# Sixteen short sequences of attention and a gated recurrence: the softmax division moved from the token layout to the layout of the values product

## The chip, the cores and the metric

One core of one Trainium2 chip. The metric is the device time of one execution in microseconds (us), the median of several runs.

## The reference

For 16 sequences of 512 tokens with 256 features, fp32: sliding-window attention with 16 heads of 16 features (window 128, so each block of 128 queries sees its own and the previous block of keys, with a bias of slope times distance), a softmax, the output projection, the residual and a LayerNorm. Then a recurrence over the 16 sequences with 512 x 256 state, and at last a hidden layer for all sequences that needs the final state, with a second residual and LayerNorm:

```python
p = softmax(where(valid, q @ k.T / sqrt(16) + slope * delta, -inf));  o = p @ v
x = layernorm(x + o @ w_out.T)
f = sigmoid(x_t @ wf.T + c @ uf.T + bf); i = sigmoid(x_t @ wi.T + c @ ui.T + bi)
g = tanh(x_t @ wc.T + c @ uc.T + bc);    c = f * c + i * g
out = layernorm(x + tanh(x @ wo.T + c_final @ uo.T + bo))
```

## The kernel before

Everything is done in 3 passes of fp32r parts: each operand is split into a high part (ScalarE copies it with rounding, "hi") and a rest (VectorE or GpSimd subtracts, "lo"), and a product is hi*hi + hi*lo + lo*hi (`product` L916, and `abreast` L924, which runs two products beside each other on the upper and lower half of the rows).

The order is written out by hand: each engine has one function `iteration(t)`, and semaphores tie them. `iteration(t)` has 16 slots, `attend(0)` to `attend(15)`. On TensorE a slot issues `raw_scores(t, ...)` (L939) for four heads of a head group g = slot // 4 and `scores` (L961) for the slot seven earlier. VectorE (`maxima` L682) takes the row maxima of the raw scores, which stand in two PSUM banks; the raw scores of the next slot wait for them (`red_done`). ScalarE takes exponentials (`exps` L441), GpSimd masks them (`window` L343), and `values` (L977) multiplies with V. Maxima travel: `max_transpose` (L957), `max_row` (L450, ScalarE), `max_to_stack` (L257, two DMAs into the rows of Qs).

Three sequences are under way in one iteration: attention of t, the rest of the attention of t - 1 and its output of t - 2, gates of t - 3. Between slots TensorE does one other thing, in the four PSUM banks A0, A1, B0, B1 (they change roles each iteration, `pairs_of` L195): slot 0 `max_transpose`, `values(t-1, 1)`, a context transpose and the `o_transpose`s; slots 1, 2 gates; 3, 4 output projection; 5 values, context transpose, the first query/key pair of t + 1 (`project_qk`); 6, 7 gates; 8 values, context transpose; 9, 10 the values projection (`v_halves`); 11, 12 the second query/key pair (`qk_halves`); 13 `values(t, 0)`, context transpose, `x1_transpose`s; 14, 15 gates.

The values product of head group g is a bank of 128 rows (4 heads of 32 rows: 16 of context, one with the softmax denominator, the rest unused) by 512 tokens. `ctx_out` (L456, ScalarE) copies it to `ctx_raw`; `ctx_transpose` (L991) turns it in four 128 x 128 transposes to token rows; `normalise` (L693, VectorE) takes reciprocals and multiplies into `o_tok`. When all four groups are there `o_transpose` (L1024) turns `o_tok` back, four transposes for each of two chunks, and `ot_hi`/`ot_lo` split it to `oT` for the projection `project_out`/`out_halves`.

The DMA queue of SyncE (`iteration` L269) sends the query/key parts to DRAM (`parts_to_dram` L232, four DMAs for each of two chunks), fetches them replicated to the stacks Qs and Ks (`stack` L242, eight DMAs a head group, `stacked[g]`), moves the maxima, and loads and stores x, xt and x1. `x_hi`/`x_lo` split the transposed input for the sequence after next in slots 1 and 2; `x_lo` (L671) is on VectorE.

Before the loop the weights are split (`STAGED` L161, `weights_hi` L411, GpSimd L338 to L341). After it `last_sequences` drains the pipeline, and a second loop of 16 steps does the hidden layer.

## Time and profile before

| | us |
|---|---|
| median of 3 runs (lowest, highest) | 994.1 (992.67, 994.81) |
| the profiled execution | 994.83 |
| its span, first to last instruction | 992.7 |
| busy: TensorE, its weight loads, VectorE, ScalarE, GpSimd | 911.2, 749.7, 714.1, 574.8, 409.0 |
| mean granted clock of TensorE | 0.955 of full |

The profiled execution gives all durations; its own time is 2.1 us more than its span. "PEld" is the loading of weights on TensorE, one per matmul, and runs beside the previous matmul; the starts of these loads give the order and pace in which TensorE issues.

### The profile page before, as it was taken

To read this page: it belongs to the slowest core of one execution; us is meant where nothing else is said; L and a number is where in the kernel's file an instruction comes from. 1 tells how busy PE (TensorE), PEld (TensorE's weight loads), DVE (VectorE), ACT (ScalarE), POOL (GpSimd) and SP (SyncE) were. 2 spreads that over 40 slices of the span, in tenths; PEclk is the share of its full clock that TensorE was granted. 3 is DMA by queue.
4 is the path that set the end of the run, shared out by engine and by line. 5 is a ranking of instruction groups with operands and counts; after the bars stand their busy time and mean duration, and the time that the engine had idled before them with its cause. 6 is when DMAs were issued, how large, how long until landed. Compare 5 with 4: busy or idle time off the path is not lost. (4 is left out here: it accounts for less than half of the span.)

```text
span 992.7 us, 25986 instructions
## 1 busy us (share of the span) xinstructions
PE 911.2 (92%) x9500; PEld 749.7 (76%) x9500; DVE 714.1 (72%) x2795; ACT 574.8 (58%) x1167; POOL 409.0 (41%) x687
## 2 busy tenths in 40 slices
PE   3587889999999999999999999999999999989994
PEld 2365668888888888888888888888787876668884
DVE  7666677878787868787878787878787754337875
ACT  6044556565656565656565656565656554335786
POOL 6143343444535353535353535354444443001443
PEclk8586989999999999999999999999999989899998
DMA  7644454535454545353645454645444400131764
GB/s 265 164 124 127 131 139 132 151 122 156 124 151 128 145 134 150 123 154 125 153 128 151 128 143 137 149 131 147 133 121 138 119 23 22 44 106 46 215 204 131
DMA packets 93534, 131.86 MB, mean 133 GB/s; under 512 B 12128, under 2 KB 47584, under 8 KB 93408
## 3 DMA queue, kind: packets, MB, share of 16 engines
q1 hardware_dynamic: 93136, 129.95, 45.3%
q8 instruction: 76, 1.25, 0.5%
q14 instruction: 50, 0.41, 0.1%
q10 hardware_dynamic: 272, 0.26, 0.1%
HBM read 79.31 MB, written 50.33 MB: 131 GB/s over the span
## 5 line engine op out<-in xcount | busy, mean ns | idle before, releaser
L689 DVE CUSTOM_DVE_ANT_0 bank<-bank,mask 128x256 f32<-128x256 f32 (+1 forms) x1024 | 369.4, 423 | 130.7 <-PE bank L951 128.7
L448 ACT ACTIVATE Pt<-bank 128x512 f32<-128x512 f32 (+1 forms) x512 | 248.2, 536 | 193.4 <-PE bank L972 193.3
L347 POOL TENSOR_SCALAR_AFFINE_SELECT Pt<-Pt 128x512 f32<-128x512 f32 x256 | 170.4, 666 | 403.9 <-ACT Pt L448 403.9
L951 PE MATMUL bank<-Ks,Qs 59*128 59x256 f32 (+1 forms) x1024 | 148.2, 319 | 44.9 <-DVE max_q L689 31.3
L951 PEld LDWEIGHTS bank<-Ks,Qs 59*128 59x128 f32 x1024 | 107.3, 191 | 86.6 <-DVE max_q L689 42.5
L689 DVE DVE_READ_ACCUMULATOR2_ANT max_q<- 128x1 f32 x1024 | 144.9, 142 | 0.0
L349 POOL TENSOR_SCALAR_AFFINE_SELECT Pt<-Pt 128x384 f32<-128x384 f32 x256 | 144.7, 565 | 0.0
L986 PE MATMUL bank<-Pt,Vp 128*32 128x256 f32 (+1 forms) x2048 | 130.9, 377 | 0.0
L932 PE MATMUL bank<-x1T,Wg 64*128 64x512 f32 x960 | 127.9, 398 | 1.0 <-DVE o_tok L703 1.0
L932 PE MATMUL bank<-cT,Ug 64*128 64x512 f32 x960 | 125.7, 393 | 0.0
L972 PE MATMUL bank<-Qs,Ks 60*128 60x256 f32 (+1 forms) x1024 | 111.8, 271 | 0.7 <-ACT Pt L448 0.3
L986 PEld LDWEIGHTS bank<-Pt,Vp 128*32 128x32 f32 x2048 | 81.4, 116 | 31.9 <-issue 7.9
L932 PEld LDWEIGHTS bank<-cT,Ug 64*128 64x128 f32 x960 | 89.1, 184 | 18.2
L932 PEld LDWEIGHTS bank<-x1T,Wg 64*128 64x128 f32 x960 | 87.3, 185 | 18.9 <-DVE o_tok L703 1.4
L972 PEld LDWEIGHTS bank<-Qs,Ks 60*128 60x128 f32 x1024 | 94.7, 192 | 3.0 <-issue 1.3
L459 ACT ACTIVATE ctx_raw<-bank 128x512 f32<-128x512 f32 x64 | 38.2, 597 | 53.3 <-PE bank L994 50.7
L486 ACT ACTIVATE gate<-bank,bias_half 128x512 f32<-128x512 f32 x64 | 42.4, 685 | 42.2 <-PE bank L932 23.9
L920 PE MATMUL bank<-xT,Win 128*128 128x512 f32 x204 | 55.1, 423 | 7.9 <-DVE Win L661 7.9
L932 PE MATMUL bank<-Win,xT 64*128 64x256 f32 x768 | 54.6, 284 | 0.0
L920 PEld LDWEIGHTS bank<-xT,Win 128*128 128x128 f32 x204 | 40.1, 203 | 16.6 <-DVE Win L661 7.9
L661 DVE SCALAR_TENSOR_TENSOR qk_parts<-bank,qk_parts 128x512 fp32r<-128x512 f32 x64 | 42.5, 685 | 13.9 <-ACT qk_parts L431 13.9
L431 ACT ACTIVATE qk_parts<-bank 128x512 fp32r<-128x512 f32 x64 | 38.0, 593 | 23.0 <-PE bank L920 20.2
(111 smaller groups left out, 1354.7 us busy)
## 6 DMA issues: line engine op xcount, KB each, us to landing
parts_dram<-qk_parts SPq DMA_DIRECT2D x128, 256.0 KB
Qs<-parts_dram SPq DMA_DIRECT2D x128, 128.0 KB, 2.7
Ks<-parts_dram SPq DMA_DIRECT2D x128, 128.0 KB, 2.8
xt_raw<-in_xt SPq DMA_DIRECT2D x16, 512.0 KB, 4.5
Qs<-parts_dram SPq DMA_DIRECT2D x128, 64.0 KB, 2.7
Ks<-parts_dram SPq DMA_DIRECT2D x128, 64.0 KB, 2.7
x_res<-in_x SPq DMA_DIRECT2D x16, 512.0 KB, 3.9
x_dram<-y SPq DMA_DIRECT2D x16, 512.0 KB, 4.4
```

The source lines that it names most:

```text
L347: gp.affine_select(out=p4[:, :, 0:128], in_=p4[:, :, 0:128], compare_op=ALU.is_ge, fill=0.0, base=0, pattern=[[0, 4], [1, 128]], channel_m ...
L349: gp.affine_select(out=p4[:, 0:3, 128:256], in_=p4[:, 0:3, 128:256], compare_op=ALU.is_ge, fill=0.0, base=0, pattern=[[0, 3], [-1, 128]], ...
L448: sc.activation(probabilities(g, 2 * pair + odd)[:, S * a:S * a + n], SC[odd][:, 0:n], ACT.Exp).then_inc(exp_done, 1)
L459: sc.activation(ctx_raw[:, :], bank[:, :], ACT.Copy).then_inc(ctx_done, 1)
L486: ins = sc.activation(gate[:, k if k == 3 else which, :], bank[:, :], ACT.Tanh, bias=bias_half[:, which, j:j + 1], scale=0.5)
L661: return ve.scalar_tensor_tensor(out_, in_, scale, hi.bitcast(F32), op0=ALU.mult, op1=ALU.subtract)
L689: ins = ve.tensor_tensor_reduce(out=raw, in0=raw, in1=mask[:, keys], scale=1.0, scalar=MASKED, op0=ALU.add, op1=ALU.max, accum_out=max_q[: ...
L920: ins = te.matmul(out_, w, m, start=(first and n == 0), stop=(last and n == len(todo) - 1))
L932: ins = te.matmul(out_, w(r), m(r), start=(turn == 0 and opens and n == 0), stop=final, skip_group_check=True)
L951: ins = te.matmul(MX[odd][:, 256 * (n % 2):256 * (n % 2) + 256][:, keys], Qs[rows, 2 * g + pair, n * WIN:(n + 1) * WIN], Ks[rows, 2 * g + ...
L972: ins = te.matmul(SC[odd][:, 256 * (j % 2):256 * (j % 2) + width], Ks[rows, 2 * g + pair, j * WIN:(j + 1) * WIN], Qs[rows, 2 * g + pair, j ...
L986: ins = te.matmul(bank[32 * hh:32 * hh + 32, j * WIN:j * WIN + width], Vp[:, j, PITCH * h:PITCH * h + 32], probabilities(g, hh)[:, 256 * j ...
```

## The change

Division happens in the layout of the values product, for all sequences but the last (whose old path stays, as `last_ctx_transpose`, `last_normalise`, `last_o_transpose`, `last_ot_hi`, `last_ot_lo`):

- `ctx_out` waits for its own copy and sends `ctx_raw` to DRAM (`ctx_dram`) from ScalarE's queue.
- SyncE loads the contexts back as `o_un`, 128 rows of context a chunk (`load_contexts`), and the denominators as `den_q` (`load_denominators`, four DMAs). VectorE transposes `den_q` in blocks, inverts, transposes back; SyncE stores the inverses and loads them replicated over the 16 rows of each head as `inv_den`; GpSimd multiplies (`scale_contexts`). `ot_hi` and `ot_lo` read `o_un` from SBUF.
- `ctx_transpose`, `normalise` and `o_transpose` go.
- `x_hi`/`x_lo` are now for t + 2, in slots 13 to 15, and `x_lo` is on GpSimd, between its windows 1 and 2 of group 1.
- The values projection and the second query/key pair change places (slots 9, 10 and 11, 12) and banks; slots 0, 13 and 14 use the other pair of banks, and in slot 13 the x1 transposes come ahead of `values(t, 0)`.
- `parts_to_dram(t, 1)` moves from the end of iteration t - 1 behind `stack(t, 1)` of iteration t; `max_to_stack(t, 0)` ahead of `stack(t, 2)`.
- Wo and Uo take the place of Win in SBUF and are loaded and split at the end of the loop.

```diff
@@ SyncE
+            def load_denominators(t):
+                sp.wait_ge(den_cleared, 1)
+                for g in range(QUADS):
+                    wait(sp, ctx_stored[g], 16, t, 16)
+                wait(sp, inv_stored, 16, t - 1, 16)
+                rows = ctx_dram[t % 2].rearrange("g (h r) (q i) -> q (g h) r i", r=2 * D, i=128)[:, :, D, :]
+                for q in range(4):
+                    sp.dma_start(den_q[32 * q:32 * q + H, :], rows[q]).then_inc(den_in, 16)
+            def load_contexts(t, c):
+                for g in (2 * c, 2 * c + 1):
+                    wait(sp, ctx_stored[g], 16, t, 16)
+                wait(sp, otlo_done, 2, t - 1, c + 1)
+                rows = ctx_dram[t % 2, 2 * c:2 * c + 2].rearrange("g (h r) s -> (g h) r s", r=2 * D)[:, 0:D, :]
+                sp.dma_start(o_un[:, c, :], rows).then_inc(o_un_in[c], 16)
+            def store_inverses(t):
+                wait(sp, inv_turned, 1, t, 1)
+                sp.dma_start(inv_dram[t % 2].rearrange("r (q i) -> q r i", i=128), den_q[:, :]).then_inc(inv_stored, 16)
+            def spread_inverses(t):
+                wait(sp, inv_stored, 16, t, 16)
+                for c in range(KC):
+                    wait(sp, scaled_done, 2, t - 1, c + 1)
+                    rows = inv_dram[t % 2, 8 * c:8 * c + 8]
+                    sp.dma_start(inv_den[:, c, :], rows.unsqueeze(1).to_broadcast([8, D, S])).then_inc(inv_in[c], 16)
...
+                by_rows = p1 and t - 1 < B - 1
                 if p1: max_to_stack(t - 1, 3)
-                if now: stack(t, 1)
+                if now:
+                    stack(t, 1)
+                    if t: parts_to_dram(t, 1)
...
+                if by_rows: load_contexts(t - 1, 0)
                 if real(t + 2): load_xt(t + 2)
                 if now:
+                    max_to_stack(t, 0)
                     stack(t, 2)
-                    max_to_stack(t, 0)
                     stack(t, 3)
...
+                if by_rows: load_denominators(t - 1)
                 if n1: stack(t + 1, 0)
+                if by_rows: load_contexts(t - 1, 1)
                 if now: max_to_stack(t, 2)
-                if n1: parts_to_dram(t + 1, 1)
+                if by_rows:
+                    store_inverses(t - 1)
+                    spread_inverses(t - 1)
+                if t == B - 1: load_last_weights()
@@ GpSimd
+                if p2 and t - 2 < B - 1:
+                    for c in range(KC):
+                        scale_contexts(t - 2, c)
                 if p1:
...
+                    for hh in range(2):
+                        window(t, 1, hh)
+                    if real(t + 2):
+                        for c in range(KC):
+                            x_lo(t + 2, c)
+                    for hh in range(2, 4):
                         window(t, 1, hh)
@@ ScalarE
                 sc.activation(ctx_raw[:, :], bank[:, :], ACT.Copy).then_inc(ctx_done, 1)
+                if t < B - 1:
+                    wait(act, ctx_done, 4, t, g + 1)
+                    sc.dma_start(ctx_dram[t % 2, g], ctx_raw[:, :]).then_inc(ctx_stored[g], 16)
...
                 attend(10)
+                if n1: qk_hi(t + 1, 2, A0)
                 attend(11)
-                v_out(t, 0, A0)
+                if n1: qk_hi(t + 1, 3, A1)
                 attend(12)
-                v_out(t, 1, A1)
-                if n1: qk_hi(t + 1, 2, B0)
-                max_row(t, 2, A0)
+                v_out(t, 0, B0)
+                v_out(t, 1, B1)
+                if p2: x1_hi(t - 2, 0, A0)
+                max_row(t, 2, B0)
                 attend(13)
-                if n1: qk_hi(t + 1, 3, B1)
-                ctx_out(t, 0, A1)
-                if p2:
-                    x1_hi(t - 2, 0, B0)
-                    x1_hi(t - 2, 1, B1)
+                if p2: x1_hi(t - 2, 1, A1)
+                ctx_out(t, 0, B1)
+                if real(t + 2): x_hi(t + 2, 0)
                 attend(14)
+                if real(t + 2): x_hi(t + 2, 1)
@@ VectorE
                 attend(10)
+                if n1: qk_lo(t + 1, 2, A0)
                 attend(11)
+                if n1: qk_lo(t + 1, 3, A1)
                 attend(12)
-                if n1: qk_lo(t + 1, 2, B0)
                 attend(13)
-                if n1: qk_lo(t + 1, 3, B1)
-                if p1: normalise(t - 1, 3, A0)
-                if p2:
-                    x1_lo(t - 2, 0, B0)
-                    x1_lo(t - 2, 1, B1)
+                if p1:
+                    turn_denominators(t - 1)
+                    invert_denominators(t - 1)
+                if p2: x1_lo(t - 2, 0, A0)
+                if p1: turn_inverses(t - 1)
+                if p2: x1_lo(t - 2, 1, A1)
@@ TensorE
                 attend(9)
-                v0, v1 = v_halves(t, 0, A0), v_halves(t, 1, A1)
+                if n1: q2, q3 = qk_halves(t + 1, 2, A0), qk_halves(t + 1, 3, A1)
...
                 attend(11)
-                if n1: q2, q3 = qk_halves(t + 1, 2, B0), qk_halves(t + 1, 3, B1)
+                v0, v1 = v_halves(t, 0, B0), v_halves(t, 1, B1)
...
                 attend(13)
+                if p2:
+                    x1_transpose(t - 2, 0, A0)
+                    x1_transpose(t - 2, 1, A1)
                 wait(pe, v_done, 2, t, 1)
-                max_transpose(t, 2, A0)
-                values(t, 0, A1)
+                max_transpose(t, 2, B0)
+                values(t, 0, B1)
...
                 if p2:
-                    g0, g1 = gate_halves(0, A0, state_first=True), gate_halves(1, A1, state_first=True)
-                    wait(pe, o_done, 4, t - 1, 4)
+                    g0, g1 = gate_halves(0, B0, state_first=True), gate_halves(1, B1, state_first=True)
+                    wait(pe, maxrow_done, 4, t, 3)
                     wait(pe, ctx_done, 4, t, 1)
```

## Rows read from the trace of the kernel before

**Rows 1.** The page: busy time, and the granted clock in 40 slices.
```profile
PE 911.2 (92%) x9500; PEld 749.7 (76%) x9500; DVE 714.1 (72%) x2795; ACT 574.8 (58%) x1167; POOL 409.0 (41%) x687
...
PE   3587889999999999999999999999999999989994
```
**Rows 2.** Busy time by stretches: stretch, its length, engines, clock, DMA share, GB/s.
```profile
510.00:558.00 48.00, 47.52 (x555) 39.63 (x559) 36.99 (x154) 29.48 (x63) 22.87 (x38) 1.00 0.49 145
```
**Rows 3.** Waits from 160 to 760 us: total, times, longest.
```profile
POOL Pt L347 <- ACT Pt L448: 273.8, 72, 5.3
...
PEld bank L951 <- DVE max_q L689: 13.2, 41, 0.6
```
**Rows 4.** Timeline of PEld around the transposes: start, duration, what, count.
```profile
496.97 0.42 PEld L994 LDWEIGHTS bank<-ident,ctx_raw 128*128 128x128 f32 x4 [0.20 <-issue]
497.56 0.30 PEld L951 LDWEIGHTS bank<-Ks,Qs 59*128 59x128 f32 x4 [0.17 <-issue]
...
510.03 0.42 PEld L1040 LDWEIGHTS bank<-ident,y 128*128 128x128 f32 x4 [0.35 <-DVE qk_parts L661]
...
513.76 0.43 PEld L951 LDWEIGHTS bank<-Ks,Qs 59*128 59x128 f32 x4
...
517.03 0.43 PEld L951 LDWEIGHTS bank<-Ks,Qs 59*128 59x128 f32 x4
...
519.60 0.42 PEld L994 LDWEIGHTS bank<-ident,ctx_raw 128*128 128x128 f32 x4 [0.20 <-issue]
...
521.07 0.30 PEld L951 LDWEIGHTS bank<-Ks,Qs 59*128 59x128 f32 x4 [0.17 <-issue]
...
534.49 0.42 PEld L994 LDWEIGHTS bank<-ident,ctx_raw 128*128 128x128 f32 x4 [0.20 <-issue]
534.88 2.60 PEld L920 LDWEIGHTS bank<-xT,Win 128*128 128x128 f32 x12
...
546.83 0.42 PEld L994 LDWEIGHTS bank<-ident,ctx_raw 128*128 128x128 f32 x4 [0.20 <-issue]
```
**Rows 5.** Timeline of PEld, raw scores of slots 10 to 13.
```profile
500.35 0.29 PEld L951 LDWEIGHTS bank<-Ks,Qs 59*128 59x128 f32 x3 [0.58 <-DVE max_q L689]
...
502.11 0.42 PEld L951 LDWEIGHTS bank<-Ks,Qs 59*128 59x128 f32 x4
...
504.36 0.29 PEld L951 LDWEIGHTS bank<-Ks,Qs 59*128 59x128 f32 x3 [0.30 <-DVE max_q L689]
...
504.71 1.33 PEld L932 LDWEIGHTS bank<-xT,Win 64*128 64x128 f32 x12
...
506.32 0.29 PEld L951 LDWEIGHTS bank<-Ks,Qs 59*128 59x128 f32 x3 [0.15 <-DVE max_q L689]
```
**Rows 6.** Timelines of ACT and DVE: qk_hi, qk_lo, the residual.
```profile
506.57 0.60 ACT L431 ACTIVATE qk_parts<-bank 128x512 fp32r<-128x512 f32 x1 [0.19 <-PE bank L932]
...
507.20 0.69 DVE L661 SCALAR_TENSOR_TENSOR qk_parts<-bank,qk_parts 128x512 fp32r<-128x512 f32 x1 [0.94 <-ACT qk_parts L431]
...
533.91 1.28 DVE L715 TENSOR_TENSOR y<-bank,x_res 128x512 f32<-128x512 f32 x2
```
**Rows 7.** POOL's subtraction by line; landing of stack's DMAs (L254); an issue of SP.
```profile
L364 POOL TENSOR_TENSOR cT<-c,cT x26: 1265/1280/1301, 199.7 to 798.4; 128x512 fp32r<-128x512 f32 x26
...
DMA to landing us min/median/max: 2.0/2.7/5.9
...
499.29 0.44 SPq L285 DMA_DIRECT2D x_dram<-y  x1
```
**Rows 8.** Timelines of POOL and DVE at the start of the kernel.
```profile
21.56 1.44 POOL L340 TENSOR_TENSOR Wo<-Pt,Wo 128x512 fp32r<-128x512 f32 x1
22.96 3.42 POOL L340 TENSOR_TENSOR Ug<-gate,Ug 128x1536 fp32r<-128x1536 f32 x1
...
23.04 5.57 DVE L661 SCALAR_TENSOR_TENSOR cT<-c,cT 128x512 fp32r<-128x512 f32 x2 [1.16 <-ACT cT L613]
```
**Rows 9.** Stretch of 10 us near the end, columns as in rows 2.
```profile
870.00:880.00 10.00, 8.02 (x39) 6.64 (x38) 5.44 (x14) 3.58 (x7) 1.68 (x4) 0.83 0.00 0
```

More of the change, by code:

```diff
@@ L70, in build @@
         rden = sb("rden", [128, 16])
-        o_tok = sb("o_tok", [128, NB, E])
+        o_un = sb("o_un", [128, KC, S])
+        inv_den = sb("inv_den", [128, KC, S])
+        den_q = sb("den_q", [128, 128])
+        den_t = sb("den_t", [128, 128])
+        last_o_tok = sb("last_o_tok", [128, NB, E])
         oT = sb("oT", [128, 2, KC, S], F32R)
@@ L161, in build @@
         STAGED = ((Wout, w_stage[:, 1536:2048]), (Wg, w_stage[:, 2048:3584]),
-                  (Wo, w_stage[:, 3584:4096]), (Ug, gate[:, 0:3, :].rearrange("p a b -> p (a b)")), (Uo, ctx_raw[:, :]))
+                  (Ug, gate[:, 0:3, :].rearrange("p a b -> p (a b)")))
         def real(t):
@@ L364, in c_lo, with x_lo, scale_contexts @@
                 gp.tensor_tensor(cT[:, 1, j, :], c2[:, j, :], cT[:, 0, j, :].bitcast(F32), ALU.subtract).then_inc(clo_done, 1)
+            def x_lo(t, c):
+                wait(pool, xhi_done, 2, t, c + 1)
+                gp.tensor_tensor(xT[:, t % 2, 1, c, :], xt_raw[:, c, :], xT[:, t % 2, 0, c, :].bitcast(F32), ALU.subtract).then_inc(xlo_done, 1)
+            def scale_contexts(t, c):
+                wait(pool, o_un_in[c], 16, t, 16)
+                wait(pool, inv_in[c], 16, t, 16)
+                gp.tensor_tensor(o_un[:, c, :], o_un[:, c, :], inv_den[:, c, :], ALU.mult).then_inc(scaled_done, 1)
             def iteration(t):
                 p1, p2, now = real(t - 1), real(t - 2), real(t)
+                if p2 and t - 2 < B - 1:
+                    for c in range(KC):
+                        scale_contexts(t - 2, c)
                 if p1:
@@ L384, in iteration @@
                         window(t, 0, hh)
-                    for hh in range(4):
+                    for hh in range(2):
[4 more added lines that the diff above has]
+                    for hh in range(2, 4):
                         window(t, 1, hh)
@@ L389, in _ @@
                 iteration(t)
+                if t == B:
+                    for n, w in enumerate((Wo, Uo)):
+                        pool.wait_ge(last_hi, n + 1)
+                        gp.tensor_tensor(w[:, 1, :, :], out_stage[:, n, :].rearrange("p (c n) -> p c n", c=KC),
+                                         w[:, 0, :, :].bitcast(F32), ALU.subtract).then_inc(last_lo, 1)
             def second(t, rnd, i):
@@ L605, in _ @@
             for k in range(4):
-                qk_hi(0, k, banks[4 + (k + 2) % 4])
-            act.wait_ge(weights_in, 80)
-            for n in range(5):
+                qk_hi(0, k, banks[4 + k])
+            act.wait_ge(weights_in, 48)
+            for n in range(3):
                 weights_hi(n)
@@ L762, in iteration @@
                 attend(0)
-                if p1: normalise(t - 1, 0, A0)
-                if p2:
-                    ot_lo(t - 2, 0, B0)
-                    ot_lo(t - 2, 1, B1)
-                attend(1)
-                if n1: x_lo(t + 1, 0)
-                if p3: forget(t - 3, 0)
-                attend(2)
-                if n1: x_lo(t + 1, 1)
+                if p3: forget(t - 3, 0)
+                attend(1)
+                if t == 0: x_lo(1, 0)
+                attend(2)
+                if t == 0: x_lo(1, 1)
+                if p2:
+                    ot_lo(t - 2, 0)
+                    ot_lo(t - 2, 1)
                 attend(3)
@@ L989, in values, with last_ctx_transpose @@
                 ins.then_inc(pv_ready, 1)
-            def ctx_transpose(t, g, bank):
-                wait(pe, ctx_done, 4, t, g + 1)
+            def last_ctx_transpose(g, bank):
+                wait(pe, ctx_done, 4, B - 1, g + 1)
                 for n in range(NB):
@@ L1217, in last_sequences @@
                 values(t, 2, MX[1])
[L1218 removed]
+                last_ctx_transpose(1, MX[0])
                 wait(pe, gate_done, 6, t - 2, 3)
@@ L1224, in last_sequences @@
                 scores(t, 3, 2)
-                wait(pe, o_done, 4, t, 2)
-                ctx_transpose(t, 2, MX[0])
+                pe.wait_ge(o_done, 2)
+                last_ctx_transpose(2, MX[0])
                 scores(t, 3, 3)
@@ L1236, in last_sequences @@
                 gate_of_input(t - 1, 1, A1)
-                wait(pe, o_done, 4, t, 3)
-                ctx_transpose(t, 3, MX[0])
+                pe.wait_ge(o_done, 3)
+                last_ctx_transpose(3, MX[0])
                 gate_of_state(t - 1, 0, A0)
```

237 lines of the change are left out of this document (129 added, 108 removed).

## The prediction

> **What bounds the kernel now.** I read the page first: TensorE (PE) is busy for 92% of the span, and between the first and the last slices every slice reads 9 [rows 1]. The table by stages then shows one 48 us stretch of the steady state: PE 47.5 us busy at granted clock 1.00, VectorE (DVE) 37.0, ScalarE (ACT) 29.5, POOL 22.9, the DMA engines at half [rows 2]. So what PE issues sets the pace. The waits of 160 to 760 us say how tightly: PE's weight loads (PEld) waited only 13.2 us for DVE's maxima [rows 3]. The order of these loads is the schedule. A sequence is 16 slots (the attends 0 to 15); the context transposes of slot 8 come at 496.97 and, a sequence later, at 546.83, so the period is 49.9 us [rows 4]. A full slot with gate products takes 3.27 (513.76 to 517.03 [rows 4]). The reader is to see in rows 4 what follows the transposes, and in rows 5 that slots 9 to 13 are different from the rest: there PE has little to do between two raw scores, and the loop raw scores, maxima, next raw scores sets the pace: 2.25 us for an odd slot (502.11 to 504.36), 1.96 for an even one (504.36 to 506.32).
>
> **What PE loses.** Per sequence: 16 context transposes and 8 of o_tok. Slot 0 has four and eight: 519.60 to 521.07, 1.47 us. Slot 8 has four and the change of operand behind them: 496.97 to 497.56, 0.59. In slot 5 four cost 534.49 to 534.88, 0.39, slot 13 the same [rows 4]. But in slot 5 the query/key product that follows goes into the bank that the residual reads: that addition starts at 533.91, and two take 1.28 [rows 6], so the bank is free at 534.6 and 0.28 is saved, not 0.39. In slot 13 the x1 transposes also waited 0.35 for qk_lo [rows 4], which now comes two slots earlier. Together 1.47 + 0.59 + 0.39 + 0.28 + 0.35 = 3.08 us a sequence. This is the ceiling of the gain.
>
> **What PE gets back as waits.** First the swap. The query/key pair now closes in slot 10 instead of 12, and DVE has qk_lo behind maxima 10 and 11. Today the chain reads: raw loads 504.36, product loads 504.71 to 506.04, ACT copy from 506.57, DVE qk_lo 507.20 to 507.89 [rows 5, 6]: 3.53 us from the raw loads to its end. Today only x1 transposes stand behind it. Then it is maxima 11 that stands behind it on DVE, and raw scores 12 on PE wait for those: 3.53 + (2.25 - 0.53, the lag from loads to the reader) = 5.25 us from raw 10 to raw 12, against 504.36 - 500.35 = 4.01 now: +1.24. The second qk_lo (0.69) stands before maxima 12 where the lag of 0.53 covers most: +0.16. I take 1.4 (the chain is the nearest row there is: the same instructions, two slots later); the bounds are 0 (DVE takes both in gaps) and 2 x (0.69 + 0.60) = 2.6, both copies and both subtractions in full.
>
> Second, slot 13 now ends with values(t, 0) in B1, and slot 14's gate product needs B1 empty. The copy starts 0.53 after the last load (506.04 to 506.57) and takes 0.60 [rows 5, 6]: 1.13. PE spends 0.20 on the change of operand [rows 4] and 0.35 on the scores (504.36 to 504.71) before it asks for the bank: wait 0.58. ACT is then still at the second x1 copy, which stands behind the exponentials of slot 13: half a copy more, 0.27. I take 0.85, bounds 0.58 and 1.18 (a whole copy ahead).
>
> Third, slots 0 to 3. ACT has copies of the gates, the exponentials, the context copy, its wait for that copy and a DMA issue, then ot_hi. With slot 0 shortened, the scores of slot 1 reach ACT's exponentials earlier than they end: 0.1. ot_lo of both chunks now stands between maxima 2 and 3 and reads o_un and oT, both in SBUF. Here the trace shows how POOL and DVE disturb each other: two DVE subtractions with both inputs in SBUF took 5.57 us from 23.04 while POOL ran a tensor_tensor of 3.42 from 22.96 [rows 8]; such an operation with one input in PSUM takes 0.69 [rows 6]. So DVE was held until POOL's was over. The Trainium skill ("SBUF — State Buffer", section "SBUF: two separate sides") has it that the pair of ports is an exclusive lock for the whole instruction; by that rule forget waits behind scale_contexts too, and the trace agrees. I charge 0.15 for ot_lo behind the windows; forget (slot 0) may lose up to one POOL operation, 1.28 [rows 7], but slot 1 is a slot of 3.27 with gate products as cover, so 0; without them it would be 1.28. Sum of this part 0.25, bounds 0 and 1.3.
>
> **What costs nothing, and why.** x_lo leaves DVE for POOL (two of 1.28 [rows 7]) between windows 1 and 2 of group 1; POOL sat idle 273.8 us of 600 before its windows [rows 3]. The values of slot 0 need these windows: they come last on POOL behind both x_lo, and the cover is thin, a few tenths. scale_contexts adds two more; the next windows are wanted in slot 5. If these covers went, it would be 1.28 for each x_lo. DVE loses four reciprocals, four multiplications and two x_lo, gains two transposes and one reciprocal: it is not the bound except in slots 9 to 13. ACT issues four DMAs, 0.44 each if they are like SP's [rows 7], in its idle time. DMA: 1 MB written and 1 MB read more a sequence on 7 MB, at a share of 0.49 [rows 2]. SP gets nine more issues; parts_to_dram(t, 1) moves behind stack(t, 1), wanted at slot 8; load_contexts(t-1, 0) holds SP until ot_lo in slot 2, then max_to_stack(t, 0) goes ahead of stack(t, 2), still three slots ahead of its use in slot 8. stack(t, 1) has to land before slot 4, which comes 1.5 us sooner than now, since slot 0 is shorter; its DMAs land after 2.7 [rows 7]. I put nothing down for it, as no wait for a DMA is among the large ones now; it is the cover that I know least.
>
> **The sum.** Steady state: -3.08 + 1.4 + 0.85 + 0.25 = -0.58 us a sequence, in 13 of them: -7.5. Iterations 1 and 2, at a partly lower clock and already waiting for DVE: -0.6 each, -1.2. Start: POOL has no longer Wo's 1.44 ahead of Ug [rows 8], and DVE is released to maxima 0 that much sooner: -1.4 (bounds 0 and 3.1). End: eight o_tok transposes less (1.47 - 0.39 = 1.1), three copies of the last weights (0.60 each) ahead of the layernorm that PE waits for: +0.7. Total -9.4. The profiled execution took 994.8 us (span 992.7), 0.7 above the median of 994.1. 994.8 - 9.4 = 985.4, or 984.7 from the median: I say **985**. With every wait at its low end the steady state gives 13 x (0.58 - 3.08) = -32.5, at its high end 13 x (2.6 + 1.18 + 1.3 - 3.08) = +26: 960 to 1018 with the -1.9 of both ends of the kernel. All at an end together is improbable; the forecast's own range is 974 to 996.
>
> **Rivals.** (1) *The waits are mostly covered*, DVE taking qk_lo in the pauses it has before each raw score in slots 9 to 13. For it: those pauses are 0.5 us and the period is otherwise PE's. Against: maxima 11 is in order behind it. Gain 2 to 3.08 a sequence: 994.1 - 1.9 - 13 x 3.08 = 952, or 966. Chance 0.27. (2) *The inverses land late.* After turn_inverses in slot 13: an issue 0.44, a landing 2.7, two issues 0.9, a landing 2.7 [rows 7]: 6.7 us; two slots of 3.27 and the wait of 0.85 later, at 7.4, POOL is ready for them. Its two multiplications take 2.56, ACT wants the result some 4.5 us after slot 0 began: margin about 2. With both landings at the longest, 5.9, the chain is 6.4 longer and 4 late; ot_hi then holds the exponentials of slot 2, and scores 3 and the output product wait. A third of that, 1.3 us a sequence, is what slots 2 and 3 can't hide if only one of the landings is long: 985 + 17 = 1002. It decides once the two landings take over some 7.5 us together. Chance 0.13. The Trainium skill ("DMA: Bandwidth & Descriptors", section "Why a DMA increments its semaphore by 16 and not by 1") says that a DMA is spread over the largest number up to 16 that divides both slowest dimensions; the inverse store's is 4, and the spreads' 8, so by it this would be the case to come. No row here shows engines by DMA. (3) *The clock falls*, the slower side. Where PE was busy for 8.0 of 10 us the granted clock was 0.83, a third of the time at 1.2 instead of 2.4 GHz [rows 9]. Slots 10 to 14 would have some 2 us of idle time in 12. One such drop each sequence costs up to 1.7 us: 985 + 13 x 1.7 = 1007. Against: with slots 9 to 13 as they are, the clock stays at 1.00 [rows 2]. It decides if the idle time lies together. Chance 0.10. (4) *Nothing in the net*: 992 to 996, the returned waits equal the removed work, 0.05. The forecast has 0.45.
>
> **How the numbers follow.** 0.2% of 994 is 2 us, about what a measurement can tell from no change. Faster: the forecast below 992 (0.38), rival 1 (0.27), a little of 2: 0.67. Same: 0.09. Slower: rivals 2 and 3 and the upper end of the forecast, 0.24. The range from 952 to 1007 leaves out the end of either side.
>
> **What would show it.** The period by raw-score loads: 49.3 by the forecast, 47 by rival 1. Right: slot 0 near 2.5 us, no ctx_transpose; a wait of PEld L951 for DVE's maxima of over 1 us in slot 12; a wait of PE for ACT's ctx_raw of about 0.8 in slot 14; granted clock 1.00. Rival 2 shows as POOL's scale waiting for DMA inv_den and PE for oT in slot 3; rival 3 as a clock below 1 in the steady slices. Wrong altogether: the slots 11 to 13 as short as now, or SP late with stack(t, 1) at slot 4 (PE waiting for Ks, Qs from parts_dram).

## The result, and the profile after

The changed kernel takes 1056.02 us (median of 4, 1053.76 to 1057.9), the kernel before in the same comparison 994.45 us (median of 4): ratio 1.0615, 95% interval 1.058 to 1.0649. The prediction was 985 with a range from 952 to 1007: the sign is wrong, and the time lies 49 us beyond the slower end. The profiled execution has a span of 1054.3 us, 61.6 more than before. Here and below a ratio leaves out runs that lie over 1.5% above the fastest run of their kernel (one of four in e2, three of twelve in e12; in e3 it would leave a single run, so none is given).

The page after, busy time and slices (columns as in [rows 1]):

```profile
PE 900.7 (85%) x9140; PEld 741.6 (70%) x9140; DVE 692.8 (66%) x2693; ACT 578.3 (55%) x1167; POOL 487.9 (46%) x745
...
PE   3587789898989898979898989899897989789995
...
PEclk9677789998989998989899999999999989899998
```

TensorE has 360 instructions and 10.5 us of work less (911.2 [rows 1]), and its idle time went from 81.5 us (992.7 - 911.2) to 153.6: its share of the span fell from 92% to 85%. The slices, which read 9 everywhere before, alternate between 8 and 9, and the granted clock does the same. A wait that recurs once a sequence looks like this. The waits of 160 to 800 us name it (engine, line, waited for: total, times, longest):

```profile
PEld bank L1042 <- DVE y L838: 54.8, 12, 6.1
DVE y L838 <- DMA x_res<-in_x: 48.8, 12, 5.6
POOL o_un L432 <- DMA inv_den<-inv_dram: 20.0, 21, 2.4
PEld bank L1094 <- DMA Qs<-max_rows: 7.1, 9, 1.8
```

TensorE waits in slot 5 with the query/key projection (L1042) for the bank that the residual (L838) reads, and the residual waits 4.1 us a time, in all twelve sequences, for x_res, the input rows that it adds. I priced the inverses, which are late by less than 1 us a time, and not this. SyncE's timeline of one iteration shows why x_res is late, first before, then after:

```profile
518.95 1.36 SPq L262 DMA_DIRECT2D Qs<-max_rows  x2
...
524.12 0.43 SPq L275 DMA_DIRECT2D x_res<-in_x  x1
```

```profile
446.00 1.38 SPq L275 DMA_DIRECT2D Qs<-max_rows  x2
447.48 2.60 SPq L267 DMA_DIRECT2D Qs<-parts_dram  x4
450.12 1.82 SPq L267 DMA_DIRECT2D Ks<-parts_dram  x4
452.06 3.51 SPq L252 DMA_DIRECT2D parts_dram<-qk_parts  x4
455.62 1.50 SPq L326 DMA_DIRECT2D x_res<-in_x  x1
457.24 1.29 SPq L293 DMA_DIRECT2D o_un<-ctx_dram  x1
```

Before, x_res came right behind `stack(t, 1)`, 5.2 us after the issue of the maxima; now the four DMAs of `parts_to_dram(t, 1)`, 256 KB each, stand between, and it is 9.6 us. Being issued later is only half of it. The page's lists of DMA issues give size and median time from issue to landing, first before, then after:

```profile
x_res<-in_x SPq DMA_DIRECT2D x16, 512.0 KB, 3.9
```
```profile
x_res<-in_x SPq DMA_DIRECT2D x16, 512.0 KB, 8.0
```

The same 512 KB land 4.1 us later after their issue when 1 MB of stores is ahead in the queue. So x_res loses 4.4 us at the issue and 4.1 us on the way. As the wait that is left is 4.1 us, about 4.4 of the 8.5 were slack.

The rest of the loss is the clock. Four stretches around one such wait (columns as in [rows 2]):

```profile
450.00:460.00 10.00, 9.95 (x140) 8.39 (x136) 7.49 (x34) 5.21 (x11) 5.27 (x9) 1.00 0.65 179
460.00:466.00 6.00, 0.26 (x1) 0.26 (x2) 1.00 (x2) 0.60 (x1) 0.00 (x0) 0.93 0.95 271
466.00:472.00 6.00, 6.00 (x20) 4.39 (x22) 1.88 (x10) 0.60 (x1) 1.68 (x4) 0.50 0.63 109
472.00:482.00 10.00, 10.00 (x119) 8.15 (x119) 9.20 (x34) 7.30 (x16) 4.33 (x7) 1.00 0.55 152
```

TensorE does almost nothing for 6 us (0.26 of 6.00) while the DMA engines are busy at 0.95, and is then granted 0.50, the 1.2 GHz level, for the next 6 us. The twelve loads of the query/key projection behind this wait take 4.77 us where the same twelve took 2.60 [rows 4] (over sequences 3 to 14 it is 3.57 to 4.77, on average 4.40):

```profile
465.74 4.77 PEld L1042 LDWEIGHTS bank<-xT,Win 128*128 128x128 f32 x12 [6.06 <-DVE y L838]
```

The period is read as before, from the starts of the raw-score loads: means over sequences 3 to 14, by slot. Slots 2, 3, 4, 6 and 9, left out, changed by less than 0.1.

| slots | 5 | 7 | 8 | 10 | 11 | 12 | 13 | 14 | 15 | 0 | 1 | period |
|---|---|---|---|---|---|---|---|---|---|---|---|---|
| before | 6.08 | 3.28 | 3.16 | 2.54 | 1.83 | 2.07 | 4.63 | 3.13 | 3.27 | 4.03 | 3.36 | 49.95 |
| after | 12.04 | 3.27 | 2.58 | 2.38 | 3.10 | 2.29 | 3.86 | 3.57 | 3.35 | 2.59 | 3.15 | 54.77 |

4.83 us a sequence in these twelve is 57.9 of the 61.6 in the span; 5.0 more were lost before sequence 3, and 1.4 came back behind sequence 14. Slot 5 alone lost 5.95; everything else together gained 1.12.

### The profile page after: what moved, and what is told of

The parts are those of the page before. It is cut to its first block and busy times, and to the rows that moved or that the text cites. A ratio compares the mean times of both kernels' runs of the same rounds, so it can differ in the third digit from the quotient of the medians.

```text
span 1054.3 us, 25331 instructions
## 1 busy us (share of the span) xinstructions
PE 900.7 (85%) x9140; PEld 741.6 (70%) x9140; DVE 692.8 (66%) x2693; ACT 578.3 (55%) x1167; POOL 487.9 (46%) x745
## 2 busy tenths in 40 slices
DMA packets 114232, 164.77 MB, mean 156 GB/s; under 512 B 14588, under 2 KB 52924, under 8 KB 114108
## 5 line engine op out<-in xcount | busy, mean ns | idle before, releaser
L1073 PE MATMUL bank<-Ks,Qs 59*128 59x256 f32 (+1 forms) x1024 | 151.2, 323 | 49.3 <-DVE max_q L794 32.4
L407 POOL TENSOR_SCALAR_AFFINE_SELECT Pt<-Pt 128x384 f32<-128x384 f32 x256 | 147.4, 576 | 0.0
L1042 PE MATMUL bank<-xT,Win 128*128 128x512 f32 x204 | 79.1, 563 | 60.4 <-DVE y L838 51.8
L1108 PE MATMUL bank<-Pt,Vp 128*32 128x256 f32 (+1 forms) x2048 | 127.6, 372 | 3.1 <-POOL Pt L407 3.1
L1042 PEld LDWEIGHTS bank<-xT,Win 128*128 128x128 f32 x204 | 56.4, 285 | 78.1 <-DVE y L838 55.3
L1054 PEld LDWEIGHTS bank<-cT,Ug 64*128 64x128 f32 x960 | 92.8, 184 | 20.4 <-issue 5.2
L1054 PEld LDWEIGHTS bank<-x1T,Wg 64*128 64x128 f32 x960 | 91.2, 185 | 12.8 <-issue 0.3
L412 POOL TENSOR_SCALAR var_eps<-mean_var 128x4 f32<-128x4 f32 x16 | 3.8, 240 | 132.3 <-DVE mean_var L849 132.2
L426 POOL TENSOR_TENSOR xT<-xt_raw,xT 128x512 fp32r<-128x512 f32 x28 | 35.9, 1291 | 58.3 <-ACT xT L507 58.3
L838 DVE TENSOR_TENSOR y<-bank,x_res 128x512 f32<-128x512 f32 x32 | 20.7, 686 | 57.6 <-DMA x_res<-in_x 51.7
```

Of the source, the lines that this page charges most:

```text
L407: gp.affine_select(out=p4[:, 0:3, 128:256], in_=p4[:, 0:3, 128:256], compare_op=ALU.is_ge, fill=0.0, base=0, pattern=[[0, 3], [-1, 128]], ...
L426: gp.tensor_tensor(xT[:, t % 2, 1, c, :], xt_raw[:, c, :], xT[:, t % 2, 0, c, :].bitcast(F32), ALU.subtract).then_inc(xlo_done, 1)
L1042: ins = te.matmul(out_, w, m, start=(first and n == 0), stop=(last and n == len(todo) - 1))
L1054: ins = te.matmul(out_, w(r), m(r), start=(turn == 0 and opens and n == 0), stop=final, skip_group_check=True)
L1073: ins = te.matmul(MX[odd][:, 256 * (n % 2):256 * (n % 2) + 256][:, keys], Qs[rows, 2 * g + pair, n * WIN:(n + 1) * WIN], Ks[rows, 2 * g + ...
L1108: ins = te.matmul(bank[32 * hh:32 * hh + 32, j * WIN:j * WIN + width], Vp[:, j, PITCH * h:PITCH * h + 32], probabilities(g, hh)[:, 256 * j ...
```

## The experiments

The queue theory: the DMAs that SyncE issues are served in the order of issue; the change puts bulk (parts, contexts) ahead of transfers on which TensorE or VectorE depends within a slot or two. Its rivals: the loss is the swap and the bank waits on the engines, or it is the additional bytes, whichever queue they take. In all, twelve kernels ran; ratios are to the kernel before on the same chip, whose medians were 993.4 to 995.6 and, for e4 to e6, 996.2. The expected times came true in e7 and e12 alone; e9 missed by 1.9 us, e3 with three of its four runs, the others by more.

**e1: x_res ahead of the parts** (in the kernel after)

```diff
                 if now:
                     stack(t, 1)
-                    if t: parts_to_dram(t, 1)
                 if p2:
                     wait(sp, y_done, 2, t - 3, 2)
                     sp.dma_start(x_res[:, :, :], x[t - 2].rearrange(tok, p=128)).then_inc(xres_in, 16)
+                if now and t: parts_to_dram(t, 1)
```


> The changed kernel with the x_res load issued ahead of parts_to_dram(t, 1) instead of behind it, nothing else. Queue theory (the load stands in SyncE's queue behind 1 MB of stores, is issued some 4 us later and lands after 8.0 us instead of 3.9, and the residual of slot 5 waits for it): the landing goes back to 4 to 5 us, the wait of DVE y for DMA x_res (51.7 us in 13) goes to nearly 0, slot 5 from about 12 us to about 6, the time to 975 to 985. Traffic theory (the 33 MB added by contexts and inverses slow every load): the landing stays at 6 us or more, and the time stays above 1030.

Measured: 1023.24 us, 1.0285 (1.0257 to 1.0313), where 975 to 985 was expected. Slot 5 is down to 5.82, x_res lands after 4.4 us, and half of the loss is gone; the other half is not. A new wait stands in its place, in slot 7 (6.60 instead of 3.27):

```profile
PEld bank L1093 <- DMA Qs<-max_rows: 34.6, 17, 3.9
```

**e2: parts(t + 1, 1) back at the end of the iteration**, behind the inverses (in the kernel after)

```diff
                     stack(t, 1)
-                    if t: parts_to_dram(t, 1)
...
                     spread_inverses(t - 1)
+                if n1: parts_to_dram(t + 1, 1)
```


> The changed kernel with parts_to_dram(t + 1, 1) at the end of iteration t again (behind spread_inverses). Queue theory: as e1, 975 to 985, unless max_to_stack(t, 3) now waits for the stores, which would show as PE waiting for Qs from max_rows. Traffic theory: above 1030, since no byte is gone.

Measured: 1038.6 us, 1.04 (1.0309 to 1.0491). The place of before is no longer the same place: the end of the iteration now holds the waits for the inverses, so the parts go out late. In one iteration maxima 3 are issued at 442.56, right behind the parts (438.27, 4.09 for four); before, 6.4 us lay between (559.05 and 3.33, then 568.80). TensorE waits for maxima (36.1 us) and for the stack's keys (16.3). The time alone is what the traffic theory had (above 1030).

**e3: the kernel before with only that move**

```diff
-                if now: stack(t, 1)
+                if now:
+                    stack(t, 1)
+                    if t: parts_to_dram(t, 1)
...
-                if n1: parts_to_dram(t + 1, 1)
```


> The kernel before with one part of the change alone: parts_to_dram(t, 1) behind stack(t, 1) of iteration t, ahead of the x_res load. Queue theory: the load is issued 3.5 us later and lands after about 8, so 1.5 to 2 us after the residual wants it: 1010 to 1030. Traffic theory: nothing is added here, so no change, 992 to 997.

Measured: 1038.75 us (median; its runs spread from 1021.59 to 1045.3, too far for a ratio), before 993.4. The same wait in the kernel before, from this line alone, in the run of 1038.2 us that was profiled:

```profile
DVE y L716 <- DMA x_res<-in_x: 28.0, 12, 4.1
```

x_res lands after 8.4 us instead of 3.9, slot 5 grows from 6.08 to 9.09, the period to 53.15. Nothing of the new division is in this kernel: the move alone costs 28 us by the fastest run and 45 to 52 by the other three, so from about half to five sixths of the loss. Why the fastest run is 17 us below the others is not shown; within the profiled one slot 5 varies from 7.1 to 11.6.

**e4: e1, and the DMAs of the maxima issued by ScalarE** in `max_row` instead of SyncE

```diff
@@ SyncE, max_to_stack
-                wait(sp, maxrow_done, 4, t, g + 1)
-                for odd in range(2):
...
+                return
@@ ScalarE, max_row
+                wait(act, maxrow_done, 4, t, g + 1)
+                for odd in range(2):
+                    r = 64 * odd + ROW_MAX
+                    sc.dma_start(Qs[r:r + 1, 2 * g:2 * g + 2, :].bitcast(F32),
+                                 max_rows[8 * odd:8 * odd + 8, :].bitcast(F32)).then_inc(maxrow[g], 16)
```


> The kernel of e1 with the two DMAs of max_to_stack issued by ScalarE behind its own copy instead of by SyncE; same bytes, same DMA engines, another queue. Queue theory (PE's waits for Qs from max_rows, 34.6 us in 17 in e1, come from 8 KB standing behind 1 to 1.8 MB in SyncE's queue, landing after 7 to 9 us): these waits go, the time to 980 to 990. Traffic theory (the DMA engines themselves are too busy): they stay, and the time stays within 1% of e1's 1023.

Measured: 1062.12 us, 1.0661 (1.0635 to 1.0688). The waits for max_rows are gone (0.4 us in 1), as the queue theory has it, though in a kernel that is itself slower; but ScalarE now issues eight small DMAs a sequence between its exponentials and stands behind its own waits:

```profile
L534 ACTq DMA_DIRECT2D Qs<-max_rows x128: 627/633/2536, 41.4 to 886.1; - x128
```
```profile
ACT Pt L524 <- issue: 79.4, 47, 3.3
```

So an issue of 0.63 us and the wait ahead of it cost more on ScalarE than the late landing did.

**e5: e1, with SyncE's small transfers ahead of its large ones**

```diff
-                if by_rows: load_contexts(t - 1, 0)
-                if real(t + 2): load_xt(t + 2)
                 if now:
                     max_to_stack(t, 0)
                     stack(t, 2)
-                    stack(t, 3)
-                if n1: parts_to_dram(t + 1, 0)
+                if by_rows: load_contexts(t - 1, 0)
+                if now: stack(t, 3)
+                if real(t + 2): load_xt(t + 2)
                 if now: max_to_stack(t, 1)
+                if n1: parts_to_dram(t + 1, 0)
```


> The kernel of e1 with SyncE's order changed: max_to_stack(t, 0) and stack(t, 2) ahead of load_contexts(t - 1, 0), load_xt behind stack(t, 3), max_to_stack(t, 1) ahead of parts_to_dram(t + 1, 0). Queue theory: waits for Qs from max_rows fall from 34.6 us to under 10, time 983 to 995. Traffic theory: within 1% of e1's 1023.

Measured: 1018.81 us, 1.0225 (1.0194 to 1.0255). Slots 5 and 7 are as they should be (5.82, 3.28), and the wait has moved on, to slot 15 (5.60) and, in some sequences, 11, with the same total; 983 to 995 was expected:

```profile
PEld bank L1093 <- DMA Qs<-max_rows: 34.5, 21, 3.1
DVE den_t L800 <- DMA den_q<-ctx_dram: 22.4, 13, 3.0
```

**e6: e5, and both qk_lo of the second pair behind maxima 12** (VectorE)

```diff
-                if n1: qk_lo(t + 1, 2, A0)
                 attend(11)
-                if n1: qk_lo(t + 1, 3, A1)
                 attend(12)
+                if n1: qk_lo(t + 1, 2, A0)
+                if n1: qk_lo(t + 1, 3, A1)
```


> The kernel of e5 with VectorE's two qk_lo of the second query/key pair behind the maxima of slot 12 instead of behind those of slots 10 and 11. If the term of the prediction is right (qk_lo ahead of maxima 11 costs TensorE 1.4 us in slots 11 and 12), slots 11 and 12 together fall from 5.3 us to about 4, and the time by 13 x 1.2 = 16 us against e5, less what the x1 transposes then wait for the banks (up to 0.7 a sequence): 6 to 16 us faster than e5. If the slots are long for another reason (ScalarE's copies), no change.

Measured: 1022.75 us, 1.0289 (1.0233 to 1.0344). Slots 11 and 12 fell from 5.28 (in sequences without a DMA wait) to 4.13, 1.15 of the 1.4 that my prediction put there; slot 14 took 0.77 back, and the period stayed (51.18 after 51.21). The gain of 6 to 16 us that was expected did not come. The swap's cost is real and of the size forecast, but it is not where the 61 us are.

**e7: the kernel after without the trip**. Contexts are neither stored nor loaded, denominators and inverses neither, and SyncE has its order of before. It leaves out the attention output (o_un keeps a constant); the splits, the multiplications on GpSimd, the transposes of VectorE, the swap and TensorE's order are all there.

```diff
@@ SyncE
-                if by_rows: load_contexts(t - 1, 0)
-                if by_rows: load_denominators(t - 1)
-                if by_rows: load_contexts(t - 1, 1)
-                    store_inverses(t - 1)
-                    spread_inverses(t - 1)
@@ GpSimd, scale_contexts
-                wait(pool, o_un_in[c], 16, t, 16)
-                wait(pool, inv_in[c], 16, t, 16)
+                wait(pool, otlo_done, 2, t - 1, c + 1)
@@ ScalarE, ctx_out
-                    sc.dma_start(ctx_dram[t % 2, g], ctx_raw[:, :]).then_inc(ctx_stored[g], 16)
```


> The changed kernel without the trip through DRAM: contexts, denominators and inverses are neither stored nor loaded (o_un and inv_den hold ones, so the attention output is left out of the result), and SyncE has the order of before; all compute of the change stays. If TensorE's share of the prediction is right (period 49.3 with qk_lo's 1.4 us and slot 14's 0.45 in it, some 2.4 to 2.7 us less than before in slots 0, 5, 8 and 13), the time is 955 to 975, and the whole loss of the change lies in DMAs. If the loss lies in the new order of the engines, 985 or more.

Measured: 973.48 us, 0.9779 (0.9761 to 0.9796). Waits of 160 to 800 us:

```profile
PEld bank L1064 <- DVE max_q L783: 20.9, 49, 1.4
...
PEld bank L1085 <- DMA Qs<-max_rows: 4.8, 7, 1.2
```

No wait for x_res, and the period is 48.20: on the engines the change does gain, 1.74 us a sequence. All of the loss, 82 us between e7 and the kernel after, belongs to the trip and to SyncE's order. This refutes the first rival.

**e8: e6 with still more of SyncE's order changed**: maxima 2 ahead of `stack(t + 1, 0)`, parts(t + 1, 1) between the store and the spread of the inverses, and the first half of `x1_lo` ahead of the denominators (the inverses are turned behind both halves)

```diff
-                if now and t: parts_to_dram(t, 1)
...
-                if n1: stack(t + 1, 0)
                 if by_rows: load_contexts(t - 1, 1)
                 if now: max_to_stack(t, 2)
-                if by_rows:
-                    store_inverses(t - 1)
-                    spread_inverses(t - 1)
+                if n1: stack(t + 1, 0)
+                if by_rows: store_inverses(t - 1)
+                if n1: parts_to_dram(t + 1, 1)
+                if by_rows: spread_inverses(t - 1)
```


> The kernel of e6 with parts_to_dram(t + 1, 1) sent while SyncE otherwise waits for the stored inverses, max_to_stack(t, 2) ahead of stack(t + 1, 0), and the first x1_lo ahead of the turned denominators. Queue theory: each small DMA then has little ahead of it; PE's waits for Qs from max_rows fall from 32 us to under 12, slot 14 goes back to 3.6, time 975 to 1000. If the added bytes themselves cost the time wherever they stand, 1010 or more.

Measured: 1100.05 us, 1.1044 (1.1022 to 1.1066), the slowest of all:

```profile
POOL o_un L430 <- DMA inv_den<-inv_dram: 158.9, 22, 15.4
ACT oT L551 <- POOL o_un L430: 115.5, 22, 10.7
...
PEld bank L1092 <- DMA Qs<-max_rows: 5.3, 6, 1.9
```

The maxima are on time (5.3 us), and now it is the inverses that stand behind 1 MB. They hold GpSimd, GpSimd holds ot_hi, ot_hi holds ScalarE's exponentials and so the scores of slot 3 (11.02 instead of 2.02). That is the chain of my rival 2, with the place right, and at a price of 9.0 us a sequence instead of 1.3.

**e9: the kernel before, with ScalarE storing each context bank to DRAM** (nobody reads it): 1 MB a sequence, in a queue of its own

```diff
+                pt, pg = before(t, g)
+                wait(act, ctx_stored[pg], 16, pt, 16)
                 sc.activation(ctx_raw[:, :], bank[:, :], ACT.Copy).then_inc(ctx_done, 1)
+                wait(act, ctx_done, 4, t, g + 1)
+                sc.dma_start(ctx_dram[t % 2, g], ctx_raw[:, :]).then_inc(ctx_stored[g], 16)
```


> The kernel before with one thing added: ScalarE stores each copied context bank to DRAM (1 MB a sequence on its own queue), and nobody reads it. Queue theory (only SyncE's queue order matters): within 0.5% of before, 990 to 999. Byte theory (what is on the 16 DMA engines delays the small DMAs): 1005 or more, with PE waiting for Qs from max_rows.

Measured: 1000.86 us, 1.0059 (1.0044 to 1.0074). A quarter of a megabyte behind each context copy, its four issues and ScalarE's waits for them cost 5.7 us in all, 1.9 more than the queue theory allowed. The stores' bytes cannot be the 61 us.

**e10 and e11: the loads of contexts, x_res and xt_raw issued by ScalarE** (three loads of bulk and the second half of the contexts, four issues a sequence), the maxima left with SyncE: e10 on the order of e5, e11 on SyncE's order of the kernel after

```diff
@@ ScalarE
                 max_row(t, 0, A0)
+                load_contexts(t - 1, 0)
...
                 if n1: qk_hi(t + 1, 1, B1)
+                if real(t + 2): load_xt(t + 2)
                 attend(7)
+                if p1: load_x(t - 1)
...
                 if p3: c_hi(t - 3, 1)
+                load_contexts(t - 1, 1)
                 attend(10)
```


> e1_xres_first plus the order of e5_small_first, and the loads of contexts, x_res and xt_raw issued by ScalarE (four issues a sequence) instead of SyncE; the maxima stay with SyncE. Queue theory: what SyncE held up (x_res, then the maxima of slots 11 and 15) is no longer behind these loads, the period falls from 51.2 towards the 48.2 of e7_no_trip, ScalarE pays 4 x 0.6 of which half shows: 49.5, in all 990 to 1000. Rival, the bytes (4 MB more traffic each way makes every landing longer, whichever queue): x_res and the maxima still land late, 1015 or more.

> The kernel after, SyncE's order kept as the change has it, only the loads of contexts, x_res and xt_raw issued by ScalarE. Queue theory: the wait of the residual for x_res (48.8 us in 12) goes to nothing, x_res has half a sequence to land; 512 KB of loads less stand between parts and maxima 0, so at most a wait of 1 to 2 us in slot 7: period 50.5, 1005 to 1015 against 1056. Rival, the bytes: 1040 or more.

Measured: e10 1028.98 us, 1.0359 (1.0316 to 1.0402); e11 1061.46 us, 1.0657 (1.0616 to 1.0698). Both missed, e11 by 46 us, and by their numbers the rival had both. (The "4 MB more traffic each way" of the first is a slip: the trip adds 1 MB each way a sequence.) The waits say more. In e11 none is left for x_res, slot 5 is 5.82, and one slot has nearly all that the period is above e7's, 5.45 of 5.89 us: slot 11 (8.35), with this wait:

```profile
PEld bank L1109 <- DMA Qs<-max_rows: 61.8, 12, 6.7
```
```profile
480.86 2.50 SPq L252 DMA_DIRECT2D parts_dram<-qk_parts  x4
483.99 1.36 SPq L275 DMA_DIRECT2D Qs<-max_rows  x2
```

Maxima 1 stand directly behind the 1 MB of parts(t + 1, 0), as in the kernels before and after, but here ScalarE's loads of xt and x_res, another 1 MB, run at the same time. Two stretches around these issues:

```profile
480.00:484.00 4.00, 4.00 (x55) 3.09 (x56) 3.60 (x17) 4.00 (x10) 0.00 (x0) 1.00 1.08 244
484.00:488.00 4.00, 3.56 (x44) 2.69 (x38) 3.43 (x15) 3.40 (x7) 3.60 (x5) 1.00 1.08 281
```

The DMA share reads 1.08: all engines are taken, by both queues, and the maxima, issued at 483.99, hold TensorE until 493.47. In the kernel after, behind the same parts, the share is 0.62 in the 4 us around their issue (480 to 484), and all its waits for maxima together are 7.1 us. So the rival is half right. By these rows a transfer waits for what is ahead in its own queue (e1, e3) and also for what the other queue has under way. The Trainium skill ("DMA: Bandwidth & Descriptors", section "Issuing engines are not separate DMA queues") says that DMAs of all issuing engines run on the same 16 DMA engines and interleave, and that issuing from several engines saves only the time of the issue; the share in these rows agrees with the first half. My expectation had freed the first transfer in the queue and not gone on to the next. Not all of the wait is the maxima's, though: ScalarE is held here as well, its exponentials start again at 491.66, behind its own load of the contexts ("ACT Pt L523 <- issue", 60.4 us in 24). In e10 the parts stand behind the maxima, and slot 11 (4.49) is lost otherwise: ScalarE, in order, waits in slot 9 for the store of group 3 to land before it can issue the load of the contexts, and its exponentials wait behind that (its row "ACT Pt L522 <- issue" has 39.0 us in 24).

**e12: e10 with three steps moved**

```diff
@@ ScalarE
-                load_contexts(t - 1, 1)
                 attend(10)
...
                 if real(t + 2): x_hi(t + 2, 1)
+                load_contexts(t - 1, 1)
                 attend(15)
@@ SyncE
+                if by_rows: load_denominators(t - 1)
                 if p2:
                     wait(sp, x1_done, 4, t - 2, 4)
                     sp.dma_start(x1_dram[t - 2].rearrange(tok, p=128), y[:, :, :]).then_inc(x1_out, 16)
-                if by_rows: load_denominators(t - 1)
@@ VectorE
+                if p2: x1_lo(t - 2, 0, A0)
                 if p1:
                     turn_denominators(t - 1)
                     invert_denominators(t - 1)
-                if p2: x1_lo(t - 2, 0, A0)
-                if p1: turn_inverses(t - 1)
                 if p2: x1_lo(t - 2, 1, A1)
+                if p1: turn_inverses(t - 1)
```


> e10_bulk_act_queue with three steps moved: ScalarE loads the second half of the contexts in slot 14 instead of slot 9 (there it held ScalarE and so the scores of slot 11), SyncE loads the denominators ahead of the store of x1 instead of behind it, and VectorE subtracts the first half of x1 ahead of the denominators. Queue theory: slot 11 falls from 4.71 to 3.1 and slot 14 from 4.14 to 3.6, the period from 51.2 to 49.0, in all 990 to 1000, about the kernel before; better than before only if slot 7 has no wait left. Rival, the bytes: the waits turn up at another transfer, 1015 or more.

Measured: 993.25 us (median of 12, 987.87 to 1008.03), before 995.32 (17): 0.9983 (0.9954 to 1.0012) and 1.001 by the means of all runs, so no difference that can be told. Against the kernel after that is some 63 us less, with the same 25331 instructions and the same 164.77 MB:

```profile
span 986.1 us, 25331 instructions
...
DMA packets 114232, 164.77 MB, mean 167 GB/s; under 512 B 14588, under 2 KB 52924, under 8 KB 114108
```
```profile
POOL o_un L425 <- DMA inv_den<-inv_dram: 35.1, 22, 7.0
...
PEld bank L1108 <- DMA Qs<-max_rows: 8.5, 5, 3.5
...
PEld bank L1087 <- DMA Ks<-parts_dram: 6.3, 6, 1.9
```

This is the run that decides about the bytes. By the times alone their rival had e2, e5, e8, e10 and e11; but with every byte of the trip moved the kernel comes within 20 us of e7, which moves none of them, so that is the most that they cost as such; the other 63 of the 82 are the order and the issuing engine. The profiled run is the fastest of the twelve. Its period is 48.87. Of the 0.66 that this is above e7, 0.42 is slot 7, in five sequences of twelve, where the raw scores of slot 8 wait for the keys: the queue is still late at times. Its runs spread by 20 us, more than those of any kernel here but e3. GpSimd waits up to 7.0 us for the inverses here, and ScalarE for GpSimd in turn only 2.1 us in 4. By the rule of the Trainium skill cited under e11, nothing should come of the second queue but issue time. Here e5, with one queue, takes 1.0225 of before and e12 0.9983; but e12 has more moved than the queue, and e10, which has the queue and not the three steps, takes 1.0359, so that the queue's own share of the 2.4% is not separated.

## Why the prediction was wrong

**The step that failed** is the sentence under "What costs nothing": "parts_to_dram(t, 1) moves behind stack(t, 1), wanted at slot 8". I asked when the moved step is wanted and what it is moved behind, but not what it is moved ahead of. Between its new place and the next wait stand x_res, 512 KB that the residual wants in slot 5. The term was 0. By e3, the kernel before with this move alone, it is 3.20 us a sequence (53.15 - 49.95) in a run of 1038.2 us, and by the fastest run some 2.2 (28/13, an estimate); in the kernel after, where slot 0 is shorter by 1.44 and so slot 5 comes sooner, slot 5 is 6.22 longer than in e7. About 4.2 of this is the late transfer (54.8/12, less the 0.36 that this wait has in e7 too), about 1.8 the slow clock behind it (4.40 - 2.60). It was not the only place that had been put at nothing: with x_res on time (e1), half of the loss is still there, as maxima 0 are late behind the same parts, the contexts and xt_raw.

**A second mistake** is in the same paragraph: an issue priced at 0.44 from one store, and a landing at 2.7, as if both were constants. Each of the four stores of parts took 0.88 us to issue (3.51 for four), the load of x_res behind them 1.50 where it had been 0.43, and its landing doubled (3.9 to 8.0). Price and place are not independent in a queue. In the same way the sentence "no wait for a DMA is among the large ones now" was true and told nothing: the order of before was one in which the bulk just fitted. I had called this "the cover that I know least", and gave it no chance of its own; SyncE being late stood only under what would make the prediction wrong altogether, with the stack as the victim.

**The engine side held in part.** In e7, where no transfer disturbs it, the terms for removed work and for the swap are right, and the other two waits are too high, so that the sum gained three times the forecast:

| term, us a sequence | forecast | e7 less before |
|---|---|---|
| slot 0, transposes | -1.47 | -1.44 |
| slot 8 | -0.59 | -0.58 |
| slot 5 | -0.28 | -0.27 |
| slot 13 | -0.74 | -0.87 |
| slots 11, 12, qk_lo between the maxima | +1.4 | +1.39 |
| slot 14, the bank of values(t, 0) | +0.85 | +0.44 |
| slots 0 to 3, GpSimd and ScalarE | +0.25 | -0.21 (slot 1) |
| others (slots 10, 9) | 0 | -0.20 |
| sum | -0.58 | -1.74 |

The chain for qk_lo, built from rows two slots away, was right within the table's rounding. The bank wait in slot 14 was half of what I took and below my lower bound of 0.58: the slot before and the one after take up part of it. Slot 1 got shorter, not longer. The start went the other way: sequence 3 begins 3.3 us later in e7 than before, where -2.6 was forecast. In all e7 is 20 us below before, twice the -9.4 of the prediction: with no transfer in the way the time is 973 and not 985, just outside the forecast's own range of 974 to 996.

**The rivals.** (1) that the swap's waits are covered is refuted by slots 11 and 12. (2) late inverses is not what happened (20.0 us of waits on GpSimd, which nobody waits for), but e8 shows its chain. The prediction put beside it what the Trainium skill ("DMA: Bandwidth & Descriptors", section "Why a DMA increments its semaphore by 16 and not by 1") states on the number of engines of a DMA, 4 and 8 here, and took from it that they would be late. GpSimd's waits of at most 2.4 us do not bear out a lateness that anybody waits for, and no row gives engines by DMA. (3) the falling clock came, in slot 5 and not in slots 10 to 14, and as a result of the transfer, not of the swap. Its price, 1.8 us a sequence, is near the 1.7 of that rival, by luck. None had the cause.

**What is open.** That e11's maxima would come in time without the loads of xt and x_res beside them was read from the traces, not tried by itself, and how much of its slot 11 ScalarE's own wait would keep wasn't either. How the 5.7 us of e9 divide between bytes, issues and ScalarE's waits wasn't separated. What remains between e12 and e7 is 20 us by the medians and 13.5 by the profiled spans. Of the 13.5, 5.6 are lost before sequence 3 begins, 5.1 of them in slot 15 of sequence 2 (8.39 instead of 3.27), and 5 are slot 7 of sequences 3 to 14; the rest wasn't traced.

## What to carry to other kernels

A queue of DMAs has an order of its own, like an engine. When a transfer is moved in it, walk the queue from the new place to the next idle gap, and for each transfer that now stands behind it ask who wants it and when; price issue and landing by rows taken behind the same bulk, not in an idle queue. A mean DMA share of 0.58 (after, 160 to 800 us) hides stretches at 0.95. When a critical transfer is freed, walk on: here the wait went from slot 5 to 7, to 11 and 15, and to 3, and the time came back only in e12, where small transfers mostly stood ahead of bulk and no engine had to wait long, in order, to issue one. And a stall of some us on TensorE can cost more than its length: here 4.2 us of late transfer cost 6.2, with the clock at 0.50 behind it.

## What the runs showed of the hardware

- The same load of 512 KB landed after 3.9 us (before), 4.4 (e1) and 8.0 (after, behind 1 MB of stores in its queue). Issued by ScalarE (e11, e12) it took 9.3 and 8.8, beside the other queue's traffic; it did no harm there, being issued most of a sequence ahead (at 479.7 for 524.3 in e11). The second queue changed who waits; this load landed no sooner by it.
- 6 us in which TensorE was all but idle (0.26 us busy) were followed by 6 us at a granted clock of 0.50, and then 1.00 again (after, 460 to 482 us).
- Four small DMAs of the denominators (8 KB each) were issued in 1.71 or 1.72 us in eleven iterations of fifteen in the kernel after, but in 3.57 to 5.95 in twelve of e10, right behind the parts and the store of x1: an issue too can take longer behind bulk.
- 256 KB stored from ScalarE's queue four times a sequence cost 5.7 us of 995 (e9).
